# A two-layer kernel: mixing and convolution in one visit, another order of step and beginning, and x1 moved between partitions without DRAM

## What is computed

```
layer 0:  att = softmax(mlp(cond))            # 8 weights per batch
          w_b = sum_k att[b,k] weight[k]      # a 32 x 32 matrix per batch
          c0  = w_b @ x_b + att @ bias_k
          x1  = x + c0 @ W_base.T + b_base + sum_e alpha_e (c0 @ A_e.T) @ B_e.T * 2      # 4 experts, rank 8
layer 1:  c1  = conv1d(x1, 9 taps, 4 groups of 8 channels) + cond @ c_weight.T + bias
          out = x1 + c1 @ base_W.T + lora(c1)  # the 2 best of 28 experts, rank 8
```

## Time and profile before

| | us |
|---|---|
| three runs | 397.77, 398.65, 399.16 (median 398.65) |
| the profiled execution, whole | 398.07 |
| its span, first to last instruction | 396.1 |
| TensorE busy | 378.2 (95%) |
| VectorE busy | 277.7 (70%) |
| ScalarE busy | 100.1 (25%) |
| DMA engines' mean busy share over the span | 57% |

### The profile page before, as it was taken

The page is one execution under the profiler, slowest core; times in us unless marked ns, Lnnn a source line. Parts: engine busy times, 40 slices in busy tenths (PEclk is TensorE's granted clock), DMA queues, the critical chain, the costliest instruction groups (busy, mean ns, idle before and its releaser), DMA issues.

```text
span 396.1 us, 10974 instructions
## 1 busy us (share of the span) xinstructions
PE 378.2 (95%) x4035; PEld 324.7 (82%) x4035; DVE 277.7 (70%) x906; ACT 100.1 (25%) x285; POOL 32.5 (8%) x131
## 2 busy tenths in 40 slices
PE   5997678999999999999999999999999999999996
PEld 4896557888888888888888888888888888888784
DVE  3558648777777777777777777777777777777664
ACT  6424131222222122222222222222222222222121
POOL 3039000000000000000000000000000000000000
PEclk9999899999999999999999999999999999999999
DMA  6714843656676655555567665555556766545541
GB/s 214 253 32 116 207 81 94 150 119 151 132 159 159 158 147 134 135 143 119 134 144 159 159 158 139 144 131 143 116 139 145 159 159 158 127 112 124 118 88 53
DMA packets 66109, 54.61 MB, mean 138 GB/s; under 512 B 3311, under 2 KB 52687, under 8 KB 65962
## 3 DMA queue, kind: packets, MB, share of 16 engines
q1 hardware_dynamic: 66088, 54.35, 57.4%
q10 hardware_dynamic: 2, 0.00, 0.0%
HBM read 37.30 MB, written 16.91 MB: 137 GB/s over the span
## 4 chain that ended last, share of the span: by engine, by line
PE 88%; DMA 5%; DVE 3%; issue 2%; ACT 1%; SPq 1%; DVEq 0%
PE p_hy L883 15%; PE p_hy L884 14%; PE p_hy L889 14%; PE p_y L883 9%; PE p_xm L965 8%; PE p_y L884 8%; PE p_y L889 8%; PE p_xm L911 4%; DMA win<-x_scratch 3%; PE p_xm L979 2%; PE p_xm L944 2%; DMA w_sb<-in_w 1%; DMA x_scratch<-x 1%; PE p_hy L1036 1%; PE p_y L1036 1%
## 5 line engine op out<-in xcount | busy, mean ns | idle before, releaser
L883 PE MATMUL p_y<-w_hi,xm_hi 128*128 128x292 f32 (+1 forms) x248 | 69.1, 306 | 1.3 <-DVE x L697 1.3
L884 PE MATMUL p_y<-w_lo,xm_hi 128*128 128x292 f32 (+1 forms) x248 | 65.6, 291 | 0.0
L883 PEld LDWEIGHTS p_y<-w_hi,xm_hi 128*128 128x128 f32 x248 | 47.5, 192 | 7.4 <-issue 7.3
L883 PE MATMUL p_hy<-w_hi,c_hi 128*128 128x512 f32 x124 | 49.5, 399 | 0.1
L884 PE MATMUL p_hy<-w_lo,c_hi 128*128 128x512 f32 x124 | 49.0, 395 | 0.0
L884 PEld LDWEIGHTS p_y<-w_lo,xm_hi 128*128 128x128 f32 x248 | 47.4, 191 | 0.0
L889 PE MATMUL p_y<-w_hi,xm_lo 128*128 128x292 f32 (+1 forms) x248 | 41.9, 291 | 0.7 <-DVE xm_lo L664 0.7
L765 DVE TENSOR_TENSOR g1t_lo<-p_xm,g1t_hi 113x256 fp32r<-113x256 f32 x32 | 13.6, 424 | 40.9 <-ACT g1t_hi L578 38.6
L965 PE MATMUL p_xm<-win,wc_sb 96*32 96x128 f32 x1024 | 34.6, 276 | 2.1 <-DMA win<-x_scratch 2.0
L889 PEld LDWEIGHTS p_y<-w_hi,xm_lo 128*128 128x128 f32 x248 | 35.4, 190 | 1.0 <-DVE xm_lo L664 1.0
L486 ACT CAST xm_hi<-xm 128x512 fp32r<-128x512 f32 x32 | 19.9, 620 | 59.5 <-DVE xm L659 54.9
(11 more groups left out here) (182 smaller groups left out, 675.1 us busy)
## 6 DMA issues: line engine op xcount, KB each, us to landing
win<-x_scratch SPq DMA_DIRECT2D x96, 256.0 KB, 5.2
x_scratch<-x SPq DMA_DIRECT2D x32, 260.0 KB, 2.1
x_sb<-in_x SPq DMA_DIRECT2D x32, 256.0 KB, 2.9
out<-y_sb SPq DMA_DIRECT2D x32, 256.0 KB, 3.0
w_sb<-in_w SPq DMA_DIRECT2D x4, 256.0 KB, 5.5
w_sb<-in_w SPq DMA_DIRECT2D x1, 1024.0 KB, 6.9
a_sb<-in_a SPq DMA_DIRECT2D x1, 504.0 KB, 3.8
b_sb<-in_b SPq DMA_DIRECT2D x1, 448.0 KB
```

The source lines that it names most:

```text
L883: mm(psum, lhs_hi, rhs_hi, start=start and n == 0, stop=False)
L884: mm(psum, lhs_hi, rhs_lo, start=False, stop=False)
```

## The change

The core of it; what is left out are the PSUM places, the semaphores that go with them, and ScalarE's and VectorE's beginning, which are told below.

```diff
-            for j in range(WIN // NPH):
-                rows = slice(j * NPH * GC, (j + 1) * NPH * GC)
-                sp.dma_start(win[rows, s.mod(2)], windows[s.n()][:, :, j:j + NQ]).then_inc(win_loaded[s.mod(2)], 16)
+                if s.live():
+                    after(sp, cv_mm, s, -2)
+                    for b in range(BT):
+                        rows = slice(b * CH, (b + 1) * CH)
+                        for f in range(NPH):
+                            sp.dma_start(xw[f::NPH, s.mod(2), b, :], x1[rows, s.mod(4), f, :]).then_inc(win_loaded[s.mod(2)], 16)
...
+            def conv(v):
+
+                for j in range(TAPJ):
+                    for g in range(GROUPS):
+                        for n in range(P // CH):
+                            psum = p_x[by_batch[n], g * 512 + CV0:g * 512 + XM0].rearrange("p (b m) -> p b m", b=BT)
+                            last = mm(psum, wc_sb[by_batch[g], j], xw[by_batch[g], v.mod(2), :, n * CH + j:(n + 1) * CH + j],
+                                      start=j == 0, stop=j == TAPJ - 1)
+                last.then_inc(cv_mm, 1)
...
+                low_rank_1(v + -1)
+                if not at(s, EARLY - 1):
+                    low_rank_0(s)
                 lows_1(v)
                 if (s + 1).live():
                     product(s + 1, "a")
                     product(s + 1, "b")
                 base_1(v)
+                if (s + 2).live():
+                    mixing_ready(s + 2)
+                conv_ready(v + 1)
                 transpose_g1(v)
+                if (s + 2).live():
+                    mixing(s + 2, mix_now[:, s.mod(2)])
+                conv(v + 1)
+                if (s + 1).live():
+                    transpose_g0(s + 1)
...
                 c1_transposed(v)
+                if (s + 1).live() and not late:
+                    xm_transposed(s + 1)
+                c1_low(v)
+                if not late:
+                    residual(s)
                 if (s + 1).live():
                     xm_low(s + 1)
-            base_1(v + 1, lambda: low_rank_1(v))
-            transpose_g1(v + 1)
+            base_1(v + 1, lambda: (low_rank_1(v), transpose_g1(v + 1)))
```

More of the change, by code:

```diff
@@ L448, in _, with spread @@
                                  ).then_inc(a0_done, 1)
+            def spread(n):
+                for b in range(BT):
+                    pool.tensor_copy(*raw_blocks(n, b)).then_inc(mix_rest_done, 1)
+                    pool.wait_ge(mix_rest_done, n * BT + b + 1)
+            pool.wait_ge(raw_done, 2)
+            spread(0)
+            spread(1)
             def step(s):
@@ L455, in step @@
                     pool.tensor_copy(g0s[:, 3 * L0N:K0], beta5[:, s.n(), :]).then_inc(g0_beta_done, 1)
-                    if at(s, 0):
-                        pool.wait_ge(raw_a_done, 1)
-                        pool.wait_ge(raw_b_done, 1)
                     if at(s, 0) or at(s, 1):
                         pool.wait_ge(g0_beta_done, s.c + 1)
[L461 to L465, removed]
+                    if at(s, 0):
+                        spread(2)
+                    if at(s, 1):
+                        spread(3)
+                if (s + 3).live() and not at(s, 0) and not at(s, 1):
                     t = s + 3
@@ L575, in step @@
                     nc.scalar.copy(b1_hi[:], b1_sb[:]).then_inc(b1_hi_done, 1)
[L576 to L602, removed]
+                    g1t_high(s + -LAG)
+            def step(s):
+                if s.i is None and s.c < EARLY - 1:
+                    early_step(s)
+                    return
+                if not at(s, EARLY - 1):
+                    g0_transposed(s)
+                c1_high(s + -LAG)
+                if (s + 1).live() and not at(s, EARLY - 1):
+                    xm_high(s + 1)
+                top_exponent(s + -LAG)
+                if (s + 1).live():
+                    z0_exponent(s + 1)
+                g1t_high(s + -LAG)
+            steps(act, step, 0, NT - 1, EARLY, 6)
+            v = Tile(None, NT - 2)
+            c1_high(v)
+            top_exponent(v)
+            c1_high(v + 1)
+            g1t_high(v)
+            top_exponent(v + 1)
+            g1t_high(v + 1)
         @block.vector
@@ L796, in _ @@
             V.tensor_copy(vrow[:], p_vrow).then_inc(vrow_done, 1)
+            xm_low(first)
+            xm_transposed(second)
             dve.wait_ge(beta0_done, 1)
@@ L1008, in base_1, with warm @@
                 lo_passes(y1_bank(v), full, False)
+            def warm(n):
+                for _ in range(n):
+                    mm(p_x[:, 3 * 512:3 * 512 + P], ones[:], ones[:], start=True, stop=True)
             pe.wait_ge(ones_done, 1)
-            for _ in range(5):
-                mm(p_hy[:, 0:P], ones[:], ones[:], start=True, stop=True)
+            warm(5)
             pe.wait_ge(ld_pack, 16)
```

379 lines of the change are left out of this document (193 added, 186 removed).

## The result

The changed kernel takes 424.03 us (median of 4 runs, 422.77 to 424.73) against 398.81 (397.77 to 399.16): a ratio of 1.063, 95% interval 1.061 to 1.066. The forecast was 376, its range ended at 392. What happened is rival R2, to which I gave 0.11: SyncE became the bound.

The account below looks back on a forecast made before the run. TensorE, busy 95% of the span, was taken as the bound. Loop 14.3 plus beginning 8.0 minus tail 0.5 gives 21.8 us off the profiled 398.07, so 376; own range 370 to 384, with rivals 368 to 392.

Parts of the forecast that it names:

- R2: SyncE's queue becomes the bound, from 0.60 us per issue; at 0.62 the kernel takes 406, slower than before; chance 0.11.
- SyncE's issue, 0.46: Each of the 16 transfers per tile costs SyncE 0.46 us to issue; 8.6 in all, under the 10.45 step.
- The visit, 1.09: TensorE's merged mixing and convolution, up to the next transposition: 1.09 us; the loop gains 0.55 a step, 14.3 in all.
- R4: Small matmuls don't keep their pace over 128 records: visit 1.92 and time 398, or 4.0 and about 450; chance 0.04.
- The mixing's 0.63: TensorE's separate mixing between `lows_1` and `product` costs 0.63 us per step, and all of this goes.
- What has to fit: VectorE's and ScalarE's work fits under the new step of 10.45 us; the wait before `lows_1` costs 0 to 0.3.
- R1: VectorE's queue makes every `lows_1` in the loop start 0.3 to 0.5 us late: 386; chance 0.10.
- The beginning, 8.0: Up to tile 4's g0 transposition: first `product` 3.1 us earlier, the stretch behind it 4.9 shorter, together 8.0 saved.
- The tail, 0.5: At the end, 16 issues and a landing delay the last convolution by 0.7, 0.2 is hidden: 0.5 us lost.
- R3: TensorE's longer loop body doesn't stay in place, each of five returns costs a fetch: 386 to 401 us; chance 0.05.

Follow-up runs that it names:

- with 4 transfers: The changed kernel with 4 transfers per tile instead of 16, one per batch element, same bytes and result: 398.14 us, ratio 0.998 to the kernel before.
- the run with 32 columns: The version with 4 transfers, with the convolution's second and third shift cut to 32 of their 128 columns: 389.82 us, measured once.
- two queues: The changed kernel with its 16 transfers kept, those of batch elements 2 and 3 issued by ScalarE instead of SyncE: 409.38 us, ratio 1.025.

## Why the prediction failed, step by step

- **SyncE's issue, 0.46: wrong, and alone enough to turn the sign.** Three kinds of row stood in the earlier trace rows, and the kind with SBUF on both sides, 0.62, was set aside because its row lay in the loading rush and moved more bytes. With idle engines the same kind costs 0.62 to 0.66 for 32 and for 128 rows. It measured 0.637 under way: 16 x 0.637 + 1.2 = 11.4 instead of 8.6. The price of the rest held (1.29 for 1.2), and the issue is above the point from which it decides. (My arithmetic there was off: 0.60 gives a period of 10.8, and 10.9 needs 0.606.) R2's sum for the span gives 413 at 0.637; of the 9 more, 7 come with the packets of TensorE's code, which no step of mine priced, 1.3 from a period of 11.43 for 11.39, and the rest from the start and the end.
- **The visit, 1.09: wrong, measured 1.85** (2.16 less the 0.31 of the transposition ahead). The step that failed is "a group of 16 is as fast as a group of four", 0.11 for each group: that was the spacing of starts in a burst of 32, 7 ns a record, and the 96 records of the convolution take 16 ns each. The price stood in the same rows: the mixing's whole stay of 0.43 is 27 ns a product, and 27.7 came. Rival R4 had the mechanism and, at 1.92, nearly the size: 398 for a kernel that TensorE bounds, and 398.14 came with 4 transfers. Its other end (4.0) is out. The Trainium skill's 25 ns as the least from start to start (TensorE: Matmul & The Clock Gate, "Wait — 56ns, not 53.3ns?") I rejected by that same burst. As I counted it, one record at a time, it gives 3.2 us, and the 1.85 disagree. Counted by product it would be 64 x 25 = 1.6 us, an estimate from that page, and near. It doesn't hold as a floor in either count (16 products of 32 columns start in 0.27 us, 17 ns each, in the run with 32 columns). A long series was what to ask for.
- **The mixing's 0.63 removed: right.** With 4 transfers the first `product` comes 0.48 after the lo passes (191.50 and 191.98), as forecast. The rest of the step is as worked out: 1.82 from the g0 transposition to `lows_1` (188.74 to 190.56), and 11.24 - 10.45 = 0.79 is the visit's 0.76.
- **What has to fit: right.** In the loops of the versions that TensorE bounds there is no wait for VectorE or ScalarE, but for one of 0.3 with two queues; rival R1 didn't happen.
- **The beginning, 8.0: right in the sum, 7.5, where two errors partly cancel.** With 4 transfers the g0 transposition of tile 4 comes at 64.85, forecast 64.4. The first `product` comes at 17.8, 0.8 sooner than I had it, and the stretch behind it saves 3.6 instead of 4.9; of its waits, those for the residuals (1.76 and 1.17), for c1 of tile 0 (1.06) and for w1's lo half (0.77) are there in kind and nearly in size.
- **The tail, 0.5: 1.1** with 4 transfers; with SyncE as the bound 11.7, since the last windows can't be issued before 31 others. TensorE waits 4.99 for them, and its granted clock is at half (0.51 from 394.6 to 398.0, 0.50 from 405.0 to 408.2) around that wait; what each costs isn't separated.
- **R3, the loop's code**: 18 instruction packets instead of 12, none of them between 119.2 and 359.6, so no refetch in the rounds after the first. The longer body's return costs TensorE 0.19 every fourth step (0.05 before), about 1 us in all. The real price of code was elsewhere, in SyncE's issues beside TensorE's packets.

So two terms failed, each enough to take the gain: with only the visit's error the change is worth nothing (398), and with SyncE as the bound it costs 6%.
